# Rows sent to the experts: four tiles a block in place of three, six in the last block in place of thirteen, and the last norm's power ahead of the later transfers

## What is computed

```python
def step(S, inp):                       # per sequence and head, S is 8 x 8
    k_t, q_t, v_t, beta_t, a_t = inp
    S = S * a_t[..., None, None]
    kv_mem = jnp.einsum('bhd,bhde->bhe', k_t, S)
    delta = (v_t - kv_mem) * beta_t
    S = S + k_t[..., :, None] * delta[..., None, :]
    y_t = jnp.einsum('bhd,bhde->bhe', q_t, S)
    return (S, y_t)
...
ctx = _rmsnorm(ys, norm_w) * jax.nn.silu(gate)
...
x = _layernorm(x + ctx @ Wo.T + bo)
...
routing_indices = jnp.argmax(router_logits, axis=-1)
for e in range(E):                      # E = 8, inner width 352
    ye = jnp.einsum('sbi,hi->sbh', jax.nn.silu(g) * u, down_w[e])
    out = out + jnp.where(mask, ye, 0.0)
x = _layernorm(x + out)
```

## Time and profile before

| | us |
|---|---|
| median of 3 runs | 794.63 |
| lowest and highest | 794.47, 795.85 |
| the profiled execution's own time | 792.72 |
| its span in the trace | 790.9 |
| one block of the steady part | 33.51 |
| last block, to the last state | 39.10 |
| from there to the end | about 221 |

### The profile page before, as it was taken

The page is one execution under the profiler, slowest core; times in us unless marked ns, Lnnn a source line. Parts: engine busy times, 40 slices in busy tenths (PEclk is TensorE's granted clock), DMA queues, the critical chain, the costliest instruction groups (busy, mean ns, idle before and its releaser), DMA issues.

```text
span 790.9 us, 13851 instructions
## 1 busy us (share of the span) xinstructions
PE 657.2 (83%) x3513; PEld 504.6 (64%) x3513; DVE 633.2 (80%) x1701; ACT 417.1 (53%) x1313; POOL 601.9 (76%) x758
## 2 busy tenths in 40 slices
PE   8778687988999999798998987758786779999980
PEld 3445364755757557475665746647676778999980
DVE  3899999999999999999999999997942525666430
ACT  6726456556566555755466565233223346666561
POOL 2888798989999999999999999977632344444673
PEclk9889799999989999999899999776768989999995
DMA  6733144152433525334153332226254355777630
GB/s 171 189 102 97 49 115 107 58 150 61 130 90 88 133 66 133 102 89 124 53 150 93 89 102 59 71 65 245 64 188 133 139 181 193 236 231 236 217 116 5
DMA packets 135919, 97.28 MB, mean 123 GB/s; under 512 B 95630, under 2 KB 110225, under 8 KB 135714
## 3 DMA queue, kind: packets, MB, share of 16 engines
q1 hardware_dynamic: 130514, 87.55, 38.1%
q0 software_dynamic: 4320, 8.43, 3.3%
q10 hardware_dynamic: 1008, 0.43, 0.2%
HBM read 39.80 MB, written 31.43 MB: 90 GB/s over the span
## 4 chain that ended last, share of the span: by engine, by line
PE 39%; POOL 25%; DVE 21%; issue 6%; ACT 5%; another core or an unknown queue 1%; DMA 1%; POOLq 0%; DVEq 0%; ACTq 0%
PE banks L434 11%; POOL q_prod L1308 6%; PE banks L447 5%; PE banks L750 4%; DVE banks L1903 4%; POOL u L1308 3%; DVE banks L1877 3%; POOL x_sorted L346 3%; DVE upd L1891 3%; PE banks L674 3%; DVE prod L1861 3%; PE banks L693 2%; POOL solve L1308 2%; DVE mix L1881 2%; DVE banks L1887 2%
## 5 line engine op out<-in xcount | busy, mean ns | idle before, releaser
L1308 POOL TENSOR_TENSOR q_prod<-s_keep,q_gam 128x512 f32<-128x512 f32 x128 | 140.8, 1100 | 15.4 <-ACT s_keep L1006 8.7
L1006 ACT ACTIVATE s_keep<-banks 128x128 f32<-128x128 f32 x128 | 50.2, 392 | 168.7 <-DVE upd L1891 163.7
L750 PE MATMUL banks<-q_prod,ident 128*128 128x240 f32 (+1 forms) x496 | 115.1, 387 | 21.2 <-POOL q_prod L1308 21.2
L750 PEld LDWEIGHTS banks<-q_prod,ident 128*128 128x128 f32 x496 | 95.9, 198 | 41.3 <-POOL q_prod L1308 30.9
L434 PE MATMUL banks<-xs_t,w_tile 128*128 128x128 f32 x852 | 111.8, 283 | 8.8 <-ACT xs_t L464 4.8
L543 POOL DMA_INDIRECT out<-rows_out,xs x71 | 70.1, 987 | 60.3 <-ACT rows_out L524 53.4
L1903 DVE TENSOR_REDUCE banks<-upd 128x128 f32<-128x640 f32 x128 | 105.7, 826 | 8.2 <-ACT d_keep L1010 0.9
L434 PEld LDWEIGHTS banks<-xs_t,w_tile 128*128 128x128 f32 x852 | 105.2, 199 | 10.5 <-ACT xs_t L464 5.5
L578 DVE TENSOR_TENSOR hid<-banks,silu 128x384 f32<-128x384 f32 x71 | 39.6, 557 | 80.1 <-PE banks L434 44.4
L1877 DVE TENSOR_REDUCE banks<-prod 128x64 f32<-128x576 f32 x128 | 93.6, 731 | 0.0
L1861 DVE TENSOR_TENSOR prod<-banks,k_gam 128x512 f32<-128x512 f32 x128 | 88.3, 690 | 3.4
(11 more groups left out here) (224 smaller groups left out, 1455.1 us busy)
## 6 DMA issues: line engine op xcount, KB each, us to landing
w_tile<-gate_up_we SPq DMA_DIRECT2D x71, 352.0 KB
xs<-x_sorted SPq DMA_DIRECT2D x71, 64.5 KB, 1.8
x_ct<-in_x_ct SPq DMA_DIRECT2D x16, 256.0 KB, 2.8
k_dram<-kq_s SPq DMA_DIRECT2D x16, 256.0 KB, 2.9
q_dram<-kq_s SPq DMA_DIRECT2D x16, 256.0 KB, 3.9
out<-v_s SPq DMA_DIRECT2D x16, 256.0 KB, 2.6
out<-beta SPq DMA_DIRECT2D x16, 256.0 KB, 3.6
k_h<-k_dram SPq DMA_DIRECT2D x16, 256.0 KB, 3.2
```

The costliest lines, as they stand in the source:

```text
L750: i = mm(out, ident[:, :], q_prod[m][:, d, :, 1 - m:], start=(m == 0 and d == 0), stop=(d == DH - 1), skip_group_check=True)
L1308: b.step(label, win, lambda: tt(out, x, y, op))
```

## The change

It touches POOL's order alone. `SORTED` counts four tiles a block from block 4 on, so the first of the four places in POOL's block sends one too. Blocks 4 to 14 send 44 tiles, not 33. The last block sends one tile behind each of its first four `q_prod`, none behind the next two, and two behind the seventh: 6, not 13. In the tail two tiles, not six, go ahead of the context product, and the power of the last norm comes right behind that product, ahead of the four tiles of block 13. Each of the 64 tiles is still sent once, behind the wait for its place.

```diff
-        SORTED = {w: max(3 * (w - 4), 0) for w in range(-2, NW)}
+        SORTED = {w: max(4 * (w - 4), 0) for w in range(-2, NW)}
...
                 q_times_s(w, 0)
-                sort_to(w0, w0 + 2)
+                sort_to(w0, w0 + 1)
                 q_times_s(w, 1)
-                sort_to(w0 + 2, w0 + 4)
+                sort_to(w0 + 1, w0 + 2)
                 q_times_s(w, 2)
-                sort_to(w0 + 4, w0 + 6)
+                sort_to(w0 + 2, w0 + 3)
                 q_times_s(w, 3)
-                sort_to(w0 + 6, w0 + 8)
+                sort_to(w0 + 3, w0 + 4)
                 q_times_s(w, 4)
-                sort_to(w0 + 8, w0 + 10)
                 context(p)
                 q_times_s(w, 5)
-                sort_to(w0 + 10, w0 + 12)
                 q_times_s(w, 6)
-                sort_to(w0 + 12, w0 + 13)
+                sort_to(w0 + 4, w0 + 6)
                 return
...
-                w0 = SORTED[w - 1] + 13
+                w0 = SORTED[w - 1] + 6
                 q_times_s(p, NCH - 1)
                 sort_to(w0, (NW - 3) * TW)
                 context(p)
-                sort_to((NW - 3) * TW, (NW - 2) * TW)
                 b.wait(act, "ln_ln", p)
                 mul("ln_r", p, rstd[:, :], rstd[:, :], minus_half[:, :].to_broadcast([P, TW]), ALU.pow)
+                sort_to((NW - 3) * TW, (NW - 2) * TW)
                 sort_to((NW - 2) * TW, (NW - 1) * TW)
                 sort_to((NW - 1) * TW, NW * TW)
```

## The result

The changed kernel took 802.98 us, the median of four executions (796.83, 800.46, 805.49 and 807.02 us), beside 794.55 us for the kernel before (794.16 to 795.85). The ratio is 1.0083, with a 95% interval of 1.0045 to 1.012; it is estimated from the single executions and is not the quotient of the medians, which is 1.0106 here. Executions over 1.5% above the quickest of their kernel are left out of the ratios, which concerns three near 798 us of the changed kernel in group 1 and one of 817.48 us in group 3. The forecast was 795.4 us with a range up to 799.5, so the kernel is slower than forecast. What stands out is the spread: the four executions of the kernel before keep within 1.7 us and those of the changed one cover ten.

A forecast was written before the change was run, and what follows sets the result against it. VectorE was taken to set the pace at 33.51 us a block, with POOL right behind it. Terms of +8.1 and -7.3 us gave +0.8 on the median of 794.63: 795.4 us, range 791.5 to 799.5.

The forecast's parts named there:

- Part 4: Tail: the last norm's power ahead of block 13's four transfers, worth -7.3 us, bounds -8.7 to -5.7.
- The first terms: Tail: power starts within 0.2 us of its input, TensorE's last transposition 6.2 us earlier, waiting under 1 us, clock 1.00 after.
- the 1.6 us for the clock: Tail: without TensorE's idleness the stretch from its last transposition runs at full clock, saving another 1.6 us.
- my sign: Wrong if ScalarE's rows come 7 us earlier but TensorE's first second-part expert does not, against the end of the blocks.
- Parts 2 and 3: Last block, 13 transfers to 6: nothing, bounds 0 to -2.5 us; six transfers to two ahead of the last context product: nothing.
- Part 1: Blocks 4 to 14: one more transfer each makes POOL's cycle 34.37 us against VectorE's 33.51, costing +8.1 us, bounds 5.9 to 8.7.
- What I said of the k loads: Blocks: POOL's waits for reloaded k, 3.5 us in four blocks, are no cover for the new transfer and will be gone.
- A: Slower: twelve transfers behind the power form a train holding up TensorE's signals by 4 us in the tail: 799.4 us; chance 0.22.
- B: Faster: the new transfer costs POOL next to nothing or k waits give way; part 1 0 to 2 us, 787 to 789; chance 0.09.
- C: Slightly faster: fewer transfers in the last block are worth their bound of 2.5 us: 792.9 us; chance 0.12.

The follow-up runs named there:

- group 1: Runs on one chip: the changed kernel again (791.46 us, ratio 1.0016) and its parts one by one, beside the kernel before at 788.75 us.
- group 3: Runs on another chip: the changed kernel a third time (799.22 us, ratio 1.0059) and variants of it, beside the kernel before at 796.49 us.
- group 5: Power moved, three transfers a block, on one chip: fifteen transfers in the last block 780.22 us (0.9886), six 780.76 us (0.9892), kernel before 789.78 us.
- unused product: Unneeded POOL product in blocks 4 to 14, replacing the fourth transfer: 464 columns 1.014, 576 columns 1.0127; 576 added to the power alone: 1.0079.
- three and four in turn: The changed kernel with three and four transfers in alternate blocks, 39 ahead of the last block and not 44: 798.6 us, ratio 0.9989.
- six or nine repeats: TensorE's repeated matmuls ahead of its q_prod wait, three before: changed kernel with six 1.0000, with nine 1.0125; power alone with six 0.9923.

## Why the prediction was wrong

**Part 4 was right.** Forecast -7.3 us, measured -7.8 and -7.7 (ratios 0.9901 and 0.9903), -6.9 in the changed kernel's trace. The first terms too: the power starts 0.08 us behind its input, the transposition starts at once, and the clock from there to 618.97 is 1.00. TensorE's first expert of the second part came 6.4 us earlier against the end of the blocks (651.10 - 580.88 = 70.2, before 646.49 - 569.86 = 76.6), and its wait for rows grew a little, from 4.35 to 5.14 us. Two terms were off and made up for each other: the transposition came 6.8 us earlier against the end of the blocks and not 6.2, and of the 1.6 us for the clock nothing shows at that expert; besides the longer wait for rows, the clock fell again from 628.71 to 632.12, where before's trace has no low stretch. By the letter of my sign (7 us earlier, or part 4 is wrong) it failed by 0.6 us; the runs of the part alone show that the sign was too tight.

**Parts 2 and 3 were right at nothing.** The context product behind two transfers instead of six just waits longer for y (14.16 us, before 11.19). The last block lasts 39.17 us (39.10 before), and the kernel with six transfers in it did no better than the one with thirteen (group 1) or fifteen (group 5).

**Part 1 was mis-sized, and this is the step that failed.** The forecast's +8.1 us was POOL's cycle against VectorE's. As that it holds: 34.25 us a block instead of 34.37, and +7.4 us in the quickest execution (the slot costs 34.24 - 33.14 = 1.10 us rather than 1.23). But the part alone measured +11.4 and +12.1 us (1.0145 and 1.0152), outside its bounds of 5.9 to 8.7. The step assumed that behind the new bound nothing else would move. I asked what POOL's lateness costs VectorE and did not ask what it costs TensorE, which waits for POOL's `q_prod` at the start of every block. That wait grew from 1.15 to 1.68 us in the trace of before to 2.7 to 3.2; in many blocks the clock fell right behind it; the projection, ScalarE's copy behind it, and POOL's product came later in turn. In the earlier trace rows I had used just this (an idle TensorE and half the clock after it) for the tail, and left it out of the blocks. Counted over all traces, blocks 5 to 13: with POOL as the bound and three repeats, 51 of 81 blocks have a low stretch 2.9 to 5.2 us behind their start; with three transfers a block and no unused product, 4 of 63; with three and four in turn, 5 of 9; with six or nine repeats, none of 27. So the longer wait makes the low stretch likely and not certain: the changed kernel's quickest execution has the wait in each block and the low stretch in none.

**What I said of the k loads was right in place and short in effect.** POOL's waits for k are gone in the changed kernel, as said. I dismissed them as no cover, rightly. The kernel with three and four in turn shows the other side: they keep POOL from ever getting ahead, so that a block's slack can't be saved for the next.

**The rivals.** A had the right sign, and its mechanism exists, but the twelve transfers behind the power came as three fours with 2.5 us between them, none of ScalarE's waits there was over 2.9 us, and the 4.0 us it charged to the tail were lost in the blocks. B fell with the 34.25 us blocks: the engine is taken for the transfer's whole slot, and an unused product of the same length costs the same. C fell with group 1.

**The sum by the measured parts** is 1.0145 x 0.9901 = 1.0045 and 1.0152 x 0.9903 = 1.0054, or +3.5 to +4.3 us on 794.6: 798 to 799 us. The changed kernel's three groups gave 1.0083, 1.0016 and 1.0059, on both sides of it. So of the 7.6 us by which 802.98 missed the forecast, some 3 to 4 are the mis-sized part, and the rest is how four executions happened to fall in a kernel whose executions lie up to 13.5 us apart, which is chance and not mechanism. The outcome "slower by over 0.2%" had a chance of 0.32 and should have had most.

**What beats both kernels** is the power alone, the kernel before with one operation moved: 0.990 in two groups. Fifteen transfers in the last block with it gave 0.9886, which isn't told apart from that.

## What to carry to other kernels

When a change makes another engine the bound, look up every engine that waits for the new bound, not only the old bound: here a longer wait of TensorE was followed by half the clock in 51 of 81 blocks, and what TensorE feeds then came back to the bound. The difference of two cycles is the lowest price, not the likeliest one, and a kernel that has lost its slack should be given a wide range. In a change of several parts each should be priced and run by itself, since here the good part hid two thirds of what the bad one cost.

## What was not expected of the hardware

- **Low stretches that keep in step.** With POOL as the bound they started 3 to 5 us behind the start of one block after another, 34.13 or 37.55 us apart (235.01, 272.56, 306.69, 340.82, 378.37), at a cost of up to 0.6 us, or 2.0 for those of twice the length. Of the changed kernel's three traces one has none, one has them from block 9 and one from block 11 on. In the kernel before they come as well, mostly 26 to 29 us into a block, and such blocks last 33.5 us all the same; with the power alone four of them fell 2.9 to 4.0 us into a block and made it 0.15 to 0.35 us longer.
- **A train of transfers that hides a signal.** With thirteen indirect transfers in a row on POOL, ScalarE got TensorE's sums 2.6 to 2.8 us behind the train's end and 9 to 11 us behind their making, in three traces on two chips; on two other chips the same train did nothing. With seven in a row on one of the former chips, ScalarE got the sums 2.5 us behind their making (a wait of 4.80 us where 2.31 to 4.19 is usual).
- **Chips differ by more than the change does.** The kernel before had medians of 788.8 and 789.8 us on two chips and 794.6 to 799.1 on the others. The last stage, from the first scatter to `out` to the last, takes 130.9 to 131.2 us in all six traces of these two chips and 135.9 to 142.2 us in all others (136.6 in the trace of before, 136.8 in that of the changed kernel).
